# An adaLN transformer block on one Trainium2 core: a reordering of the prologue's work on ScalarE, VectorE and GpSimd, and three swaps inside each step

## What is computed

```
x = hidden_states                               # 4 batches, 1024 tokens, 512 features, float32
mod = (silu(c) @ wmod) -> sa, ca, ga, sb, cb, gb
ga, gb: sign kept, magnitude at least 0.25
h = layernorm(x) * (1 + ca) + sa
qf, kf = h @ Wq.T, h @ Wk.T                     # rank 64, the same scores for all 16 heads
attn = softmax(qf @ kf.T)                       # per batch, 1024 x 1024
x = x + ga * ((attn @ (h @ Wv.T)) @ Wo.T)       # the kernel multiplies Wv and Wo once, ahead
h = layernorm(x) * (1 + cb) + sb
x = x + gb * (h @ sum(factors) / sqrt(8) + bias)  # 8 factors of 512 x 512
```

## Time and profile before

| | us |
|---|---|
| median of 3 runs | 455.6 (452.86 to 457.02) |
| the profiled execution's time | 454.29 |
| its span in the profile | 452.5 |
| PE busy | 441.0 (97% of the span) |
| PEld busy | 363.6 (80%) |
| DVE busy | 356.4 (79%) |
| ACT busy | 319.6 (71%) |
| POOL busy | 233.1 (52%) |
| DMA | 88.05 MB, 195 GB/s on average |

### The profile page before, as it was taken

The page is one execution under the profiler, slowest core; times in us unless marked ns, Lnnn a source line. Parts: engine busy times, 40 slices in busy tenths (PEclk is TensorE's granted clock), DMA queues, the critical chain, the costliest instruction groups (busy, mean ns, idle before and its releaser), DMA issues. The chain is left out here.

```text
span 452.5 us, 7294 instructions
## 1 busy us (share of the span) xinstructions
PE 441.0 (97%) x2118; PEld 363.6 (80%) x2118; DVE 356.4 (79%) x610; ACT 319.6 (71%) x642; POOL 233.1 (52%) x308
## 2 busy tenths in 40 slices
PE   8999996999999999999999999999999999999996
PEld 7686885888888888888888888887788888887885
DVE  5677654587887978988877978896887877999977
ACT  3676663677978676888868787876878564667761
POOL 1528337262555635466555645465555427168882
PEclk9999998999999999999999999999999999999999
DMA  8999997123477356778596366767687136758423
GB/s 324 391 407 312 218 191 112 48 81 106 141 240 225 116 188 191 250 193 251 168 255 206 116 190 218 233 189 203 181 245 219 48 121 201 215 163 280 128 83 139
DMA packets 77750, 88.05 MB, mean 195 GB/s; under 512 B 5000, under 2 KB 55944, under 8 KB 77200
## 3 DMA queue, kind: packets, MB, share of 16 engines
q1 hardware_dynamic: 73872, 80.51, 57.0%
q0 software_dynamic: 3264, 6.29, 8.0%
q10 hardware_dynamic: 576, 0.79, 0.5%
HBM read 53.49 MB, written 34.10 MB: 194 GB/s over the span
## 5 line engine op out<-in xcount | busy, mean ns | idle before, releaser
L1667 POOL TENSOR_SCALAR ve<-mv 128x1 f32<-128x1 f32 x64 | 21.1, 330 | 164.1 <-DVE mv L1304 115.2
L525 PE MATMUL ps_o<-v_hi,pt_lo 128*128 128x512 f32 x192 | 74.7, 389 | 0.0
L524 PE MATMUL ps_o<-v_lo,pt_hi 128*128 128x512 f32 x192 | 74.7, 389 | 0.0
L526 PE MATMUL ps_o<-v_hi,pt_hi 128*128 128x512 f32 x192 | 74.7, 389 | 0.0
L860 ACT ACTIVATE h_f<-x1b,mod_t 128x128 f32<-128x128 f32 x120 | 53.1, 598 | 5.5 <-DVE x1b L1322 5.3
L1189 DVE TENSOR_TENSOR h_lo<-h_f,h_hi 128x512 fp32r<-128x512 f32 x57 | 42.8, 750 | 8.9 <-ACT h_hi L832 8.6
L524 PE MATMUL ps_v<-wvo_lo,h_hi 128*128 128x512 f32 x112 | 45.5, 406 | 1.1 <-DVE h_lo L1189 1.1
L908 ACT ACTIVATE probs<-ps_s,negmax 128x1024 f32<-128x1024 f32 x32 | 35.4, 1108 | 12.7 <-DVE negmax L1248 12.1
L525 PE MATMUL ps_v<-wvo_hi,h_lo 128*128 128x512 f32 x112 | 44.3, 396 | 0.0
L526 PE MATMUL ps_v<-wvo_hi,h_hi 128*128 128x512 f32 x112 | 44.2, 394 | 0.0
L1669 POOL TENSOR_TENSOR rstd<-ve,minus_half 128x1 f32<-128x1 f32 x64 | 41.3, 646 | 5.3
(11 more groups left out here) (232 smaller groups left out, 1179.2 us busy)
## 6 DMA issues: line engine op xcount, KB each, us to landing
x_blocks<-xn SPq DMA_DIRECT2D x50, 256.0 KB, 2.7
p_blocks<-probs SPq DMA_DIRECT2D x24, 512.0 KB, 3.5
pb<-p_blocks SPq DMA_DIRECT2D x96, 128.0 KB, 3.1
x1b<-x_blocks SPq DMA_DIRECT2D x30, 256.0 KB, 2.9
result<-x_ring SPq DMA_DIRECT2D x15, 512.0 KB, 3.0
xb<-x_blocks SPq DMA_DIRECT2D x20, 256.0 KB, 2.9
x_ring<-in_x SPq DMA_DIRECT2D x18, 256.0 KB, 3.2
wmod<-in_wmod SPq DMA_DIRECT2D x4, 1024.0 KB, 15.4
```

The source lines that it names most:

```text
L524: nc.tensor.matmul(acc, a_hi, b_lo, start=first, stop=False)
L525: nc.tensor.matmul(acc, a_lo, b_hi, start=False, stop=False)
L526: return nc.tensor.matmul(acc, a_hi, b_hi, start=False, stop=last)
L1667: nc.gpsimd.tensor_scalar(ve[:, one], mv[:, u, 1:2], EPS, None, ALU.add).then_inc(ve_done, 1)
```

## The change

Nothing is added or removed but one wait; instructions change places on ACT, DVE, POOL and SP. PE's order stays as it is.

In each step: on ACT `normalize_x1(t - 1)` goes ahead of `modulate_x1(t - 2)`; on DVE `values(t + TB)` goes ahead of `turn_x(q)`; on SP `send_x(t + TB + 2)` goes ahead of `send_p(...)`. In `normalize_x1`, tile 1 now also waits until x1's tile 0 has left `xn`.

```diff
 # SP, step
+                if 12 <= t + TB + 2 < T:
+                    send_x(t + TB + 2, u)
                 if scored_in(t) is not None and not turned_by_pe(scored_in(t)):
                     send_p(scored_in(t))
-                if 12 <= t + TB + 2 < T:
-                    send_x(t + TB + 2, u)
...
 # ACT, normalize_x1
                     act.wait_ge(xt_ps, TB + 3 + t)
+                    wait(act, x2n_out, 16 * t)
...
 # ACT, step
+                if t:
+                    normalize_x1(t - 1, 1 - u, q < T)
                 if t >= 2:
                     modulate_x1(t - 2, batch_of((t - 2) // 2))
-                if t:
-                    normalize_x1(t - 1, 1 - u, q < T)
...
 # ACT, prologue
             x_row(4)
+            values_of(2)
             h_of(4)
-            qk(1)
-            values_of(2)
             x_row(5)
             x_row(6)
+            qk(1)
             h_of(5)
-            h_of(6)
+            x_row(7)
             values_of(3)
             values_of(4)
-            x_row(7)
+            h_of(6)
+            qk(2)
             copy_rows()
-            qk(2)
+            pair_q(0)
             x_row(8)
+            values_of(5)
             h_of(7)
-            values_of(5)
+            h_of(8)
             values_of(6)
-            h_of(8)
-            pair_q(0)
             qk(3)
             values_of(7)
+            normalize_x(TB + 1, 1)
             exponentials(0)
-            normalize_x(TB + 1, 1)
...
 # DVE, step
+                values(t + TB)
                 if q < T and q not in late_x_banks:
                     turn_x(q)
-                values(t + TB)
...
 # DVE, prologue
+            moments_of(6)
             values_of(1)
-            moments_of(6)
+            moments_of(7)
+            values_of(2)
             h_first(4)
+            h_second(4)
             qk(1)
-            h_second(4)
-            values_of(2)
...
 # POOL, prologue
             last_wv_rest()
+            wqk_rest()
             of_x(2, 0)
-            wqk_rest()
             of_x(3, 1)
+            add_factor(1)
             of_x(4, 0)
             of_x(5, 1)
             of_x(6, 0)
-            add_factor(1)
+            of_x(7, 1)
+            add_factor(2)
             add_factor(5)
-            of_x(7, 1)
             of_x(TB, 0)
             of_x(TB + 1, 1)
-            add_factor(2)
+            add_factor(6)
+            of_x(TB + 2, 0)
+            add_factor(7)
             add_factor(3)
-            add_factor(6)
-            add_factor(7)
-            of_x(TB + 2, 0)
             of_x1(0, 0)
+            of_x(TB + 3, 1)
             sum_factors(0)
             sum_factors(1)
             sum_factors(2)
-            of_x(TB + 3, 1)
+            sum_factors(3)
             of_x1(1, 1)
-            sum_factors(3)
```

More of the change, by code:

```diff
@@ L1068, in _ @@
             nc.scalar.activation(silu_den[:], c_sb[:], ACT.Exp, scale=-1.0).then_inc(silu_exp, 1)
+            wv_upper(2)
             wo_upper(2)
-            wv_upper(2)
             x_row(0)
@@ L1522, in _ @@
             qk(0)
+            pair_q(0)
             h_first(3)
             h_second(3)
+            moments_of(6)
             values_of(1)
-            moments_of(6)
+            moments_of(7)
+            values_of(2)
             h_first(4)
+            h_second(4)
             qk(1)
-            h_second(4)
-            values_of(2)
             h_first(5)
             h_second(5)
-            moments_of(7)
+            values_of(3)
             moments_of(8)
             moments_of(9)
-            values_of(3)
+            values_of(4)
             h_first(6)
             h_second(6)
-            values_of(4)
             bound_gates()
@@ L1543, in _ @@
             qk(2)
-            pair_q(0)
             values_of(5)
+            h_first(8)
             values_of(6)
-            h_first(8)
             h_second(8)
@@ L1550, in _ @@
             row_max(0)
+            other_columns()
             values_of(7)
-            other_columns()
             step(0)
```

## The result

The changed kernel takes 461.3 us (median of 4 runs, 460.24 to 462.55), the kernel before 455.1 in the same series (452.86 to 457.02): a ratio of 1.0143 with a 95% interval of 1.0106 to 1.0181. Forecast were 451.0, at most 455.5, so the forecast is wrong in sign. The profiled execution took 460.24 us, its span is 458.4 (before 452.5).

A forecast was written before the change was run, and what follows sets the result against it. PE was taken as the bound, with gains only where it stands still. The terms, -4.0 - 1.6 - 0.4 + 1.9 + 0 = -4.1 us, took 454.29 to 450.2; the median was put at 451.0, range 447.0 to 455.5.

The forecast's parts named there:

- (1): PE's wait at 70.34 ahead of x tile 10's transposition goes, as adds 7 and 3 move behind `of_x(10)`: gain 4.0 us.
- (2): From 68 to 80 us the granted clock returns from 0.86 to full without the standstill: gain 1.6 us.
- (4): The factors' sum comes late, so PE waits 2.3 us at step 3's transposition of P instead of 0.4: loss 1.9.
- (5): POOL's earlier adds ahead of tiles 8 and 9: tile 8's numbers by 47.5 at the latest, no loss.
- (3): Small PE waits in the prologue close as ACT and DVE make values and moments sooner: gain 0.4 us.
- rival B: POOL's adds wait behind SP's loads, tile 8 is late and PE waits near 52: 454 to 459 us, chance 0.30.
- (6): The swaps in the steps on DVE, ACT and SP stay hidden as PE is full: 0, bounds -0.5 and +1.5.
- Rival A: No new wait in step 2, factors in by 82.5 or ACT's chain has slack: -6.0, 448 to 449.5 us, chance 0.20.
- rival C: The wait at 70 stays because of another late input: about 0 to +2 us, chance 0.05.

The follow-up runs named there:

- run 9: The kernel before with the changed order of POOL's prologue alone: 451.1 us, ratio 0.992.
- run 1: The changed kernel with all three in-step swaps (SP, ACT, DVE) undone, so the changed prologue alone: 451.7 us, ratio 0.9942.
- run 10: The kernel of run 8 with POOL's add 2 moved behind the numbers of tiles 8 and 9: 449.8 us, ratio 0.989.
- run 2: The changed kernel with SP's swap alone undone, P sent ahead of x's blocks again: 453.05 us, ratio 0.9965.
- run 8: The changed prologue with DVE's swap alone in the steps, SP and ACT as before: 451.2 us, ratio 0.9885.
- run 3: The kernel before with SP's swap alone, x's blocks sent ahead of P: 462.9 us, ratio 1.0208.
- run 11: The kernel before with SP's swap, and the gates' broadcast moved ahead of x's sending: 453.9 us, ratio 0.9983.
- run 5: The kernel before with P left in place and a spare 0.5 MB write behind each sending of x's blocks: 478.1 us, ratio 1.0483.

## Why the prediction was wrong, point by point

**(1), (2) The wait at 70 and the clock.** Right in mechanism and in size. The wait is gone, the clock is 1.00, and run 9 shows that POOL's order does it by itself. From PE's row at 52 to the one of step 3 the distance falls by 4.8 us; with the 0.6 that (4) took this is 5.4, and 5.6 were forecast. (`nmr` of tile 10 ended at 70.52 + 0.39, where 69.3 was forecast; PE, later by (5), did not have to wait for it.)

**(3)** 0.4 us forecast; runs 1 and 9 (451.7 and 451.1) show nothing of ACT's and DVE's part that can be told from none.

**(4) The factors' sum.** The chain is as told, to 0.3 us: `nmr` for x1 tile 1 was forecast at 88.7, and PE's transposition of step 3 at 92.8. POOL's timeline of the changed kernel:

```profile
81.97 5.55 POOL L1751 TENSOR_TENSOR f_sum<-f_sum,wmod 128x512 f32<-128x512 f32 x4 [0.44 <-DMA f_sum<-in_factors]
...
88.70 0.26 POOL L1672 TENSOR_SCALAR nmr<-mv,rstd 128x1 f32<-128x1 f32 x1 [0.21 <-POOL rstd L1670]
```

ACT's, waiting for just that:

```profile
88.99 0.82 ACT L935 ACTIVATE xn<-x_ring,nmr,rstd 128x512 f32<-128x512 f32 x1 [0.81 <-POOL nmr L1672]
```

and PE's:

```profile
91.82 0.39 PE L526 MATMUL ps_o<-v_hi,pt_hi 128*128 128x512 f32 x1
93.09 1.06 PE L530 MATMUL ps_t<-ident,probs 128*128 128x128 f32 x8 [0.88 <-issue]
```

PE waited 1.27 - 0.23 = 1.0 us, before 0.4: a loss of 0.6 where 1.9 were told. It came later itself, since (5) had cost it 1.6 us: two losses on one path, of which the second hides behind the first. With (5) mended (run 10) the wait is 0.5 and the sums are 1 us earlier.

**(5) The adds ahead of tiles 8 and 9.** Counted as 0, it cost 1.6 us. The forecast had tile 8's numbers "47.5 at the latest"; POOL's timeline has 49.24:

```profile
37.37 1.26 POOL L1744 DMA_DIRECT2D f_sum<-in_factors  x1 [1.25 <-DMA f_sum<-in_factors]
41.40 1.19 POOL L1744 DMA_DIRECT2D f_sum<-in_factors  x1 [2.77 <-DMA f_sum<-in_factors]
44.67 2.42 POOL L1744 DMA_DIRECT2D wmod<-in_factors  x2 [2.07 <-DMA wmod<-in_factors]
...
48.98 0.26 POOL L1672 TENSOR_SCALAR nmr<-mv,rstd 128x1 f32<-128x1 f32 x1 [0.22 <-POOL rstd L1670]
```

The halves of add 1 had landed by 37.4 and 41.4 (forecast 38 for the second), and factor 4 was not in until 44.7, where 43 was the upper end. The prediction itself named the point from which it costs, 47.7, and this is 1.5 past it; PE then waited 1.97 us between starts at 51.67 and 53.64, where the same two starts lay 0.35 apart before (52.01 and 52.36). The place is rival B's, at half its size, but the mechanism is not. These are the DMA queues of the changed kernel from 34 to 37 us (columns as in the earlier trace rows; q0 is POOL's, q1 SP's):

```profile
q0 software_dynamic: 204, 0.39, 69.5%
q1 hardware_dynamic: 204, 0.39, 40.1%
```

POOL's queue did not wait for SP's to be empty: it moved nothing from 26 to 31, but here as many packets as SP's. Both are slower while they share: SP's moves 0.13 MB per us, against 0.38 in the earlier trace rows. So what failed in this term is the size of a transfer's time. The prediction took the 10.4 us from a stretch that POOL's queue had nearly to itself (97% and 112% of the engines' time from 40 to 44 and from 44 to 48 in the kernel before); the second half of add 1 took 13.8. Run 10 takes the loss back.

**(6) The steps.** This is the step that failed, and it alone makes the error: 0 forecast with bounds of -0.5 and +1.5, and 9.4 us lost from step 8 to 24. Up to it the kernel was 3.5 us ahead, where 4.1 were forecast. The text followed P: "P leaves some 2 us later", "P is turned at the end of the step: hidden". That is true, DVE hardly waits for P. It did not ask what P's 0.5 MB now stands ahead of. In SP's list the next entries are a gate, a tile and the fetch that the whole modulation of x hangs on, and in the trace of before that fetch was already the last to be waited for: DVE stood 14.4 us in 15 waits for `xb<-x_blocks`, up to 3.1 each, with PE just covered. In step 18 it took 6.4 us to the turn, and PE stood 0.42 us for `h_lo` at 315.27: one of the four steps had no margin at all. Such a row, harmless in a kernel in which PE is full, is the measure of how little more it takes. With P behind x's sending the fetch came 7.0 us behind its issue instead of 4.7 (step 12), and SP's swap alone cost 8 us.

For ACT's swap the text named the cost, 0.8 us in every second step once the cover is gone, and took ACT's mean idle time of 2.5 us in a step as cover. The mean is not the cover of the step in which x's and x1's modulations stand one behind the other: behind a wait of 2.25 us, and late by a step before, x's modulation came 1.5 us later there (run 2 against run 8), and PE lost 0.7 to 0.8 in each of three steps, 2.4 us in the changed kernel. DVE's swap is 0, as told.

The rival on the slow side had the wrong place: it put the loss near 50 us, where 1.6 of the 11 us (1.6 and 9.4) were lost. Rival A fails by the wait of (4), rival C by the missing one at 70.

## What to carry to other kernels

When a sending is moved in a queue, ask not only when it arrives but what it now stands ahead of: list what is issued between a tile's sending and the fetch that brings it back, step by step, and look at the steps with extra traffic (here a gate and a tile in four of 20) rather than at the typical one. The sum of the bytes is a first guess only: here 0.75 MB without the broadcast was quicker than 0.5 MB with it. Issue what is ready before the queue stands waiting for something that is not: here the DMA engines were empty for 2 us while P was ready, and one broadcast moved into that gap was worth 9 us. And an engine that is 100% busy has no waits to read its margin from; that margin is read from the waits of the engine that feeds it.

## What had not been expected

- A fetch of 256 KB landed 7.0 us behind its issue with 1 MB issued in the 2.5 us ahead of it (run 3), and 3.1 us with 0.75 MB in 2.6 us (run 11), in the same step. What is missing in the second is the gates' broadcast; in the kernel before, with 0.5 MB in between but the broadcast in it, it was 4.7.
- The wait with its clock drop at 70 us is in each kernel that keeps the old order of POOL (3.8 us before, 3.7 in run 3, 4.4 in run 5, 4.6 in run 11), and in none that has the new one.
- 0.5 MB more of writes a step, of no use to anyone, cost 1.1 us a step (run 5), some 0.3 of it by the clock, though the share of the DMA engines from 100 to 300 went only from 0.65 to 0.75: the mean share says little of a queue that is full for a few us of each step.
